# State-space scan: the exponent banks from one 96-row product each over a block-diagonal operand, copies stored as often as used, and another spacing of the banks over the steps

## The chip, the core and the metric

The kernel runs on one core of one Trainium2 chip, in one launch. The metric is the device time of that launch in microseconds (us), lower is better. The engines are TensorE (PE in the profile, its weight loads PEld), VectorE (DVE), ScalarE (ACT) and GpSimd (POOL). SyncE (SP) issues most of the DMAs. The engines run their own instruction streams and wait for each other on semaphores.

## The reference

The model adds six stages to a residual `x` of 2048 tokens by 128 features: a mixture of eight GELU experts, attention, the GELU mixture again, a mixture of eight ReLU experts, a state-space scan, and the ReLU mixture again. The change is in the scan alone (and in a memory clear inside the ReLU mixture before it). The scan, cut to what matters:

```python
x = L0_attn_x
x = x + 0.5 * _L0_ffn_ref(_layernorm(x), ...)      # GELU mixture
x = x + _L0_attn_ref(_layernorm(x), ...)
x = x + 0.5 * _L0_ffn_ref(_layernorm(x), ...)
x = x + 0.5 * _L1_ffn_ref(_layernorm(x), ...)      # ReLU mixture
x = x + _L1_attn_ref(_layernorm(x), ...)           # the scan
x = x + 0.5 * _L1_ffn_ref(_layernorm(x), ...)

def _L1_attn_ref(x, norm_w, x_proj_w, dt_proj_w, dt_proj_b, A_log, D, out_proj_w):
    xn = _rmsnorm(x, norm_w)
    proj = jnp.einsum('bld,pd->blp', xn, x_proj_w)
    delta_lo, Bs, Cs = jnp.split(proj, [DT_RANK, DT_RANK + STATE], axis=-1)
    delta = jax.nn.softplus(jnp.einsum('blr,dr->bld', delta_lo, dt_proj_w) + dt_proj_b)
    A = -jnp.exp(A_log)
    # the tokens are cut into M chunks of CHUNK = 64; all chunks are stepped at once
    def step(h, inp):
        dt, bt, ct, xt = inp
        dA = jnp.exp(dt[..., None] * A)
        h = dA * h + dt[..., None] * bt[:, None, :] * xt[..., None]
        y = jnp.einsum('mdn,mn->md', h, ct)
        return (h, y)
    _, ys = jax.lax.scan(step, jnp.zeros((M, Dm, STATE)), (dt_seq, b_seq, c_seq, x_seq))
    return jnp.einsum('bld,od->blo', y + x * D, out_proj_w)
```

## The kernel before

The scan walks 64 steps (`NSTEP`), for all chunks at once. The state lies in SBUF as 128 partitions (two batch halves of 64 state entries) by 2048 columns (16 chunks by 128 features), in three buffers `hsf`. The names `usf`, `bsf`, `decayf`, `hsf`, `cz`, `aw` and most of the staging are carved out of one tile, and the profile calls all of them `arena`; `ps` is PSUM, eight banks of 512 columns. A **step** t does this:

- *inputs* (line 1042): PE forms b times u for step t+1, sixteen 12-row products into PSUM banks 0 to 3, eight for banks 0 and 1 (`inputs(e, t+1, (0, 1))`), eight for 2 and 3. 12 rows are three bfloat16 parts paired so that the product is near fp32.
- *add_input* (2025): DVE adds PSUM to the state, 1024 columns, then 512, then 512.
- *decay_state* (2037 on DVE for the first 1024 columns, 1606 on POOL for the other two times 512): state times decay, for step t+1. DVE's order in a step is add 0, add 1, multiply of t+1, add 2.
- *state_out* (1057): PE contracts the state with c, 32 instructions, into banks 6 and 7.

Four steps are a **unit** (`TU = 4`), sixteen units in all. The decay of a unit, exp(-dt A) for 4 steps, is 128 by 8192 values in `decayf[u % 2]`. It is made in 16 **banks** of 512 columns: *spread_bank* (1029) has PE form dt times A for 8 features in PSUM bank 4 or 5, and *decay_bank* (1326) has ACT take the exponent into `decayf`. A spread waits until the exponent two banks before it is done, because only two PSUM banks take turns. Before, a bank is eight products of 64 columns, each with its own weights (`aw[0:nk, d]`, 120 rows of which 12 are not zero), and the moving operand `dts` holds 10 features in its rows for 8 steps (`TC = 8`, `DG = 10`).

The order of the work is written out by hand in `scan_tensor`, `scan_scalar`, `scan_vector` and `scan_pool`. A step of PE is: the first spread of its list, inputs of banks 0 and 1, two spreads, wait for DVE's add 2, inputs of banks 2 and 3, state_out, the rest of the list. The list has 5 banks in steps 0 to 3 and 4 afterwards, so that unit u+1 is complete after step 4u+2 and the multiply for step 4u+4, issued by DVE in step 4u+3, finds it. ACT takes the exponents in the same order, and beside them, once in a unit, `state_copy` (1344), `state_place` (1353, four small copies) and `place_c` (1337, two copies); the last two stand behind the exponents of the second step of a unit.

Before the steps, `dt`, `u` and `b` are split into three bfloat16 parts (ACT casts 1385, 1386, 1391), written to DRAM by SP (631, 634, 638, 646, 652) and read back in the row arrangement that PE wants (642, 644 and `fetch_dt` 626; `fetch_inputs` 618, 24 DMAs for four steps). They all go on one SP queue. The parts lie in memory that the scan uses again: the second `decayf` holds the parts of u and b, so that the exponents of unit 1 wait for `u_out` (line 1320 of the listing), and a state buffer lies on the parts of dt, so that the first multiply waits for `dt_out`.

```python
                sp.wait_ge(SC["dt_cast"], NPART * NTB)       # line 632
...
                sp.dma_start(scratch["dt"].rearrange("d k r n -> d (k r n)"),       # line 646
                             dtparts.rearrange("p k a b n -> p (k a b n)")).then_inc(dt_out, 16)
```

## Time and profile before

| | |
|---|---|
| time, median of 3 runs | 1384.51 us (1381.24 to 1386.95) |
| the profiled execution: span from first to last instruction | 1389.3 us |
| PE busy in the span | 1105.4 us, 80% |
| DVE busy | 939.3 us, 68% |
| ACT busy | 775.9 us, 56% |
| POOL busy | 754.5 us, 54% |
| mean granted TensorE clock, share of full speed | 0.860 |

The trace gives no other time for the profiled execution than its span. The times of a trace are counted from the first instruction. Each view groups instructions by engine and line; "idle" is the time in which the engine did nothing before an instruction, with the releaser that ended it (`<-ACT arena L1326` means that it waited for ACT's line 1326). `x16` counts instructions that stand together as one row, and the duration is then that of the group. A matmul's duration includes its way through the array, so that neighbours overlap; the distance from start to start tells what it occupies. PEclk is the granted TensorE clock: 1.00 is 2.4 GHz and 0.50 is 1.2 GHz. An idle stretch of an engine matters only where something waits for what it does next.

### The profile page before, as it was taken

The page shows a single profiled execution, that of the slowest core. Times are in us where ns is not written, and L with a number is a line of the kernel's source. Part 1 is how long each engine was busy: PE and PEld are TensorE (multiplying, and loading weights), DVE is VectorE, ACT ScalarE, POOL GpSimd, SP SyncE. Part 2 cuts the span into 40 slices and gives each one's busy share as a digit, 9 for nine tenths or more (in the row PEclk, how much of TensorE's full clock was granted, in tenths as well). Part 3 has the DMA queues.
Part 4 walks back from the last instruction along what each step waited for, and adds up shares of the span by engine and source line. Part 5 has one row for each costly group of instructions (what it writes and reads, how often), then busy time and mean ns, then how long its engine had stood idle before and what let it go on. Part 6 is the DMA issues. An engine that isn't in the chain of part 4 may idle for free. (4 is left out here: it accounts for less than half of the span.)

```text
span 1389.3 us, 26829 instructions
## 1 busy us (share of the span) xinstructions
PE 1105.4 (80%) x9728; PEld 712.6 (51%) x9728; DVE 939.3 (68%) x2104; ACT 775.9 (56%) x1511; POOL 754.5 (54%) x659
## 2 busy tenths in 40 slices
PE   5899998588888888688999969553688888884783
PEld 4677775122222222266788746322566666654562
DVE  7867867777777776478777723456578888885332
ACT  6868864136565666677877714236555665541231
POOL 4876686643332321188667661623378888781322
PEclk9999999559898979899999989775779999875896
DMA  8200000301211110011000012103311111101122
GB/s 238 67 17 1 1 1 0 61 6 26 31 31 31 32 31 0 1 61 61 1 1 1 0 60 67 51 6 119 81 38 39 41 39 40 32 14 67 58 78 65
DMA packets 92154, 55.39 MB, mean 40 GB/s; under 512 B 54253, under 2 KB 85749, under 8 KB 91128
## 3 DMA queue, kind: packets, MB, share of 16 engines
q1 hardware_dynamic: 89975, 49.48, 13.4%
q0 software_dynamic: 2048, 4.20, 1.0%
q8 instruction: 79, 1.29, 0.4%
q14 instruction: 52, 0.42, 0.1%
HBM read 31.06 MB, written 14.20 MB: 33 GB/s over the span
## 5 line engine op out<-in xcount | busy, mean ns | idle before, releaser
L1606 POOL TENSOR_TENSOR arena<-arena 128x512 f32<-128x512 f32 x126 | 214.7, 1724 | 87.0 <-ACT arena L1326 35.8
L1643 POOL TENSOR_TENSOR hr<-arena,hr 128x512 fp32r<-128x512 f32 x128 | 183.2, 1439 | 63.3 <-ACT hr L1226 61.8
L782 PE MATMUL ps<-xp,wup 128*128 128x512 f32 x768 | 196.3, 406 | 15.2 <-POOL wup L1617 8.5
L1326 ACT ACTIVATE arena<-ps 128x512 f32<-128x512 f32 x256 | 142.9, 597 | 108.1 <-PE ps L1029 103.7
L782 PE MATMUL ps<-hr,wdn 128*128 128x512 f32 x768 | 196.1, 404 | 8.2 <-issue 5.5
L1226 ACT ACTIVATE arena<-ps 128x512 f32<-128x512 f32 x256 | 160.0, 625 | 75.7 <-PE ps L782 75.4
L1282 ACT ACTIVATE arena<-ps 128x1024 f32<-128x1024 f32 (+1 forms) x192 | 149.1, 810 | 89.9 <-PE ps L935 88.7
L1892 DVE TENSOR_TENSOR hr<-arena,hr 128x512 fp32r<-128x512 f32 x128 | 132.3, 1048 | 74.3 <-ACT hr L1226 74.1
L782 PEld LDWEIGHTS ps<-xp,wup 128*128 128x128 f32 x768 | 147.2, 195 | 49.4 <-POOL wup L1617 10.7
L2025 DVE TENSOR_TENSOR arena<-arena,ps 128x1024 f32<-128x1024 f32 x189 | 154.2, 857 | 18.1 <-PE ps L1042 17.7
L782 PEld LDWEIGHTS ps<-hr,wdn 128*128 128x128 f32 x768 | 143.7, 189 | 39.0 <-issue 11.2
L1226 ACT ACTIVATE hr<-ps 128x512 fp32r<-128x512 f32 x256 | 162.1, 633 | 0.0
L1958 DVE CUSTOM_DVE_ANT_0 arena<-ps,arena 128x512 f32<-128x512 f32 (+3 forms) x256 | 112.8, 488 | 58.7 <-PE ps L920 57.3
L1527 POOL TENSOR_SCALAR_AFFINE_SELECT arena<-arena 128x512 f32<-128x512 f32 x64 | 40.9, 639 | 204.3 <-ACT arena L1282 203.7
L920 PE MATMUL ps<-arena 64*128 64x512 bf16 (+3 forms) x384 | 114.6, 394 | 40.9 <-DVE maxima L1958 15.5
L920 PEld LDWEIGHTS ps<-arena 64*128 64x128 bf16 x384 | 28.5, 99 | 173.9 <-DVE maxima L1958 94.8
L950 PE MATMUL ps<-arena 128*32 128x512 f32 (+3 forms) x768 | 93.9, 566 | 5.0 <-POOL arena L1527 5.0
L2037 DVE TENSOR_TENSOR arena<-arena 128x1024 f32<-128x1024 f32 x63 | 77.6, 1232 | 27.6 <-ACT arena L1326 27.6
L935 PE MATMUL ps<-arena 64*128 64x512 bf16 (+3 forms) x384 | 89.6, 378 | 7.9 <-ACT arena L1282 7.9
L1650 POOL TENSOR_TENSOR arena<-arena 128x512 f32<-128x512 f32 x56 | 74.3, 1327 | 36.4 <-DVE arena L1907 27.0
L1961 DVE TENSOR_REDUCE maxima<-ps 128x1 f32<-128x512 f32 x128 | 81.6, 684 | 13.6 <-PE ps L920 12.6
L1669 POOL DMA_INDIRECT arena<-ys_rows,slot_of x32 | 30.3, 947 | 101.8 <-DMA ys_rows<-arena 93.3
(239 smaller groups left out, 1885.0 us busy)
## 6 DMA issues: line engine op xcount, KB each, us to landing
arena<-up_dram SPq DMA_DIRECT2D x16, 256.0 KB, 3.0
arena<-dn_dram SPq DMA_DIRECT2D x16, 256.0 KB, 3.4
ys_rows<-arena SPq DMA_DIRECT2D x8, 320.0 KB, 2.5
arena<-up_dram SPq DMA_DIRECT2D x2, 1024.0 KB, 4.8
arena<-dn_dram SPq DMA_DIRECT2D x2, 1024.0 KB, 6.9
arena<-xs_rows SPq DMA_DIRECT2D x4, 512.0 KB, 4.8
b_parts<-arena SPq DMA_DIRECT2D x1, 1536.0 KB, 5.1
dt_parts<-arena SPq DMA_DIRECT2D x1, 1536.0 KB, 6.4
```

The lines of the kernel that those rows point to most:

```text
L782: mm = e.matmul(out, left(a), right(b), start=(first and n == 0), stop=(last and n == 2))
L920: mm = e.matmul(ps[:, n % 2, m * w:(m + 1) * w], qT[vp][rows, i, h // HP, :], kT[v % 3][rows, 4 * half:4 * half + w // P, h // HP, :], sta ...
L935: mm = e.matmul(ps[:, 2 + 2 * pair + h, 0:w], kT[v % 3][rows, j, pair, :], qm[rows, vp, pair, half * 512 + q0:half * 512 + 512], start=Tru ...
L950: mm = e.matmul(ps[32 * h:32 * h + 32, 6 + half, q0:512], vpad[:, vp, j, h, :], probT[:, n % 2, h, 0:w], start=(j == 0), stop=(w == P), sk ...
L1226: a = e.activation(to, ps[:, fc, :], ACT.Gelu)
L1282: e.activation(probT[:, m % 2, 2 * pair:2 * pair + 2, 0:w], ps[:, 2 + 2 * pair:4 + 2 * pair, 0:w], ACT.Exp, scale=SCALE).then_inc(AT["exp_ ...
L1326: e.activation(to, ps[:, 4 + n % 2, :].rearrange("p (d m t) -> p t m d", d=DBK, t=TU), ACT.Exp, scale=-1.0).then_inc(SC["decay_ready"], 1)
L1606: e.tensor_tensor(hsf[t % 3][:, cols], decayf[u % 2][:, t4 * W + cols.start:t4 * W + cols.stop], hsf[(t - 1) % 3][:, cols], ALU.mult).then ...
L1643: e.tensor_tensor(hr[:, i % 2, 1, fc, :], hid[:, i % 2, fc, :], hr[:, i % 2, 0, fc, :], ALU.subtract).then_inc(MX["rest_pool"], 1)
L1892: e.tensor_tensor(hr[:, i % 2, 1, fc, :], hid[:, i % 2, fc, :], hr[:, i % 2, 0, fc, :], ALU.subtract).then_inc(MX["rest_vector"], 1)
L1958: ins = e.tensor_tensor_reduce(masked_s[n % 2][:, m * w:(m + 1) * w], of, causal[:, 4 * P - w:4 * P], 1.0, MASKED, ALU.add, ALU.max, to)
L2025: e.tensor_tensor(to, to, of, ALU.add).then_inc(SC["added"], 1)
```

## The change

- *A bank is one product.* Bank g of a unit holds the features 8g to 8g+7. The moving operand `dts` of a bank is now 96 rows (8 features by 12 rows, `BR`) by 512 columns, block-diagonal: feature l's 12 rows are filled in the columns of feature l alone and are zero elsewhere. The weights `aw[0:96, g]` hold the 8 features under each other. One matmul of 512 columns takes the place of eight of 64.
- *dt is fetched per unit.* `fetch_dt(u)` is 8 DMAs of 12 rows by 16 banks by 64 elements, in two slots that were both cleared before (the clear in the ReLU mixture covers `dts` now, and no longer all of `aw`). Before, `fetch_dt(k)` was 30 DMAs for two units, and the first read (642, 644) filled two units.
- *Rows are stored as often as used.* The DRAM copies of dt, u and b have 12 rows in place of 6: parts 0 to 2, 0 to 1 and 0 are written one after the other (`for c0, na in RUNS`). So each of these stores is 3 DMAs and twice the bytes (u twice 3), and a read is one DMA per row group: `fetch_inputs` is 8 DMAs in place of 24, of the same bytes.
- *Spacing.* `ahead_at(t)` gives a step's list: 5, 5, 5, 1 over the steps of a unit (6 in step 0). In the last step of a unit the one bank stands behind state_out. On ACT `state_place` and `place_c` move to the last step of the unit, ahead of its exponent.

The core of the diff:

```diff
-        aw = carve(D * P // 2).bitcast(BF16).rearrange("p (d n) -> p d n", n=P)
-        dts0 = carve(NDG * NM * TC // 2)
+        awf = carve(BKU * P // 2)
+        aw = awf.bitcast(BF16).rearrange("p (g n) -> p g n", n=P)
+        dtsf = carve(2 * BKU * 512 // 2)
+        dts = dtsf.bitcast(BF16).rearrange("p (s g n) -> p s g n", s=2, g=BKU)
+        assert top[0] == CLEARED
...
                 def fetch_inputs(k):
                     for r in range(RG):
                         m2, hh = r // 2, r % 2
+                        for to, name, landed in ((usf, "u", u_in), (bsf, "b", b_in)):
+                            of = scratch[name][m2, TI * k:TI * (k + 1), :, hh, :]
...
+                            sp.dma_start(to[k % 2][32 * r:32 * r + KR].rearrange("p (t n) -> p t n", t=TI),
+                                         of.rearrange("t r n -> r t n")).then_inc(landed[k % 2], 16)
...
+                def fetch_dt(u):
+                    for dl in range(DBK):
+                        sp.dma_start(dts[KR * dl:KR * (dl + 1), u % 2, :, dl * NM * TU:(dl + 1) * NM * TU],
+                                     scratch["dt"][dl::DBK, u].rearrange("g r n -> r g n")).then_inc(dt_in[u % 2], 16)
+
+                def put_dt(u0, u1, landed):
+                    for c0, na in RUNS:
+                        sp.dma_start(scratch["dt"][:, u0:u1, 2 * c0:2 * c0 + 2 * na, :].rearrange("d u r n -> d u (r n)"),
+                                     dtparts[:, u0:u1, 0:na].rearrange("p k a b n -> p k (a b n)")).then_inc(landed, 16)
+
+                def put_u(t0, t1, landed):
+                    for m2 in range(2):
                         for c0, na in RUNS:
-                            rows = slice(32 * r + 2 * c0, 32 * r + 2 * c0 + 2 * na)
-                            for to, name, a0, landed in ((usf, "u", 0, u_in), (bsf, "b", NPART - na, b_in)):
-                                of = scratch[name][m2, TI * k:TI * (k + 1), a0:a0 + na, :, hh, :]
-                                sp.dma_start(to[k % 2][rows].rearrange("p (t n) -> p t n", t=TI),
-                                             of.rearrange("t a b n -> (a b) t n")).then_inc(landed[k % 2], 16)
-
-                def fetch_dt(k):
-                    for dg in range(DG):
-                        ng = len(range(dg, D, DG))
-                        for c0, na in RUNS:
-                            r0 = KR * dg + 2 * c0
-                            sp.dma_start(dts[k % 2][r0:r0 + 2 * na, 0:ng, :],
-                                         scratch["dt"][dg::DG, k, 0:2 * na, :].rearrange("g r n -> r g n")
-                                         ).then_inc(dt_in[k % 2], 16)
+                            sp.dma_start(scratch["u"][m2, t0:t1, 2 * c0:2 * c0 + 2 * na].rearrange("t r h n -> t (r h n)"),
...
+                put_dt(0, 2, dt0_out)
...
+                put_u(0, TI, stored)
                 sp.wait_ge(dt0_out, 16 * len(RUNS))
...
+                sp.wait_ge(SC["zeroed"], 2)
+                fetch_dt(0)
+                sp.wait_ge(b_out, 16 * len(RUNS))
+                sp.wait_ge(stored, 16 * U_STORES)
                 fetch_inputs(0)
...
+                put_dt(2, NUN, dt_out)
+                put_u(TI, CHUNK, u_out)
+                fetch_dt(1)
+                sp.wait_ge(u_out, 16 * 2 * len(RUNS))
                 fetch_inputs(1)
-                sp.wait_ge(dt_out, 16)
-                sp.wait_ge(SC["xn_turned"], NTB)
-                fetch_dt(1)
-                for k in range(2, NI):
-                    sp.wait_ge(SC["in_done"], 3 * TI * (k - 1))
-                    fetch_inputs(k)
-                    if k % 2 == 0 and k // 2 + 1 < NC:
-                        sp.wait_ge(SC["spread_done"], 2 * BKU * (k // 2))
-                        fetch_dt(k // 2 + 1)
+                sp.wait_ge(dt_out, 16 * len(RUNS))
+                for k in range(1, NI):
+                    if k >= 2:
+                        sp.wait_ge(SC["in_done"], 3 * TI * (k - 1))
+                        fetch_inputs(k)
+                    if k + 1 < NUN:
+                        sp.wait_ge(SC["spread_done"], BKU * k)
+                        fetch_dt(k + 1)
...
         def spread_bank(e, n):
 
-            u, q = unit_of(n)
-            k, th = u * TU // TC, u % (TC // TU)
-            if q == 0 and th == 0:
-                e.wait_ge(dt_in[k % 2], 16 * 2 if k == 0 else 16 * (2 - 2 * (k % 2) + DG * len(RUNS) * ((k + 1) // 2)))
+            u, g = unit_of(n)
+            if g == 0:
+                e.wait_ge(dt_in[u % 2], 16 * DBK * (u // 2 + 1))
             if n >= 2:
                 e.wait_ge(SC["decay_ready"], n - 1)
-            for j in range(DBK):
-                d = q * DBK + j
-                nk = KR * min(DG, D - d // DG * DG)
-                of = dts[k % 2][0:nk, d // DG, :].rearrange("p (m t) -> p m t", t=TC)
-                mm = e.matmul(ps[:, 4 + n % 2, j * 64:(j + 1) * 64], aw[0:nk, d, :],
-                              of[:, :, th * TU:(th + 1) * TU], start=True, stop=True)
-            mm.then_inc(SC["spread_done"], 1)
+            e.matmul(ps[:, 4 + n % 2, :], aw[0:BR, g, :], dts[0:BR, u % 2, g, :], start=True, stop=True).then_inc(SC["spread_done"], 1)
+
+        def ahead_at(t):
+
+            first = 0 if t == 0 else 5 * (t % TU) + 1
+            first += BKU * (t // TU + 1)
+            return [n for n in range(first, first + (6 if t == 0 else 1 if t % TU == TU - 1 else 5)) if n < NUN * BKU]
...
-            ahead = BKU
             for t in range(NSTEP):
-                todo = [n for n in range(ahead, ahead + (5 if t < 4 else 4)) if n < NUN * BKU]
-                ahead += len(todo)
-                for n in todo[0:1]:
+                todo = ahead_at(t)
+                last = t % TU == TU - 1
+                for n in todo[0:1] if not last else ():
                     spread_bank(e, n)
                 if t + 1 < NSTEP:
                     e.wait_ge(SC["added"], 3 * t + 1)
                     inputs(e, t + 1, (0, 1))
-                for n in todo[1:2]:
-                    spread_bank(e, n)
-                for n in todo[2:3]:
+                for n in todo[1:3] if not last else ():
                     spread_bank(e, n)
                 e.wait_ge(SC["added"], 3 * t + 3)
                 if t + 1 < NSTEP:
                     inputs(e, t + 1, (2, 3))
                 state_out(e, t)
-                for n in todo[3:]:
+                for n in todo if last else todo[3:]:
...
+                u, t4 = t // TU, t % TU
+                todo = ahead_at(t)
+                if t4 == TU - 1:
+                    if u >= 1:
+                        state_place(e, u - 1)
+                        if u + 1 < NUN:
+                            place_c(e, u + 1)
+                for n in todo[0:3]:
                     decay_bank(e, n)
-                if t % TU == 0 and t > 0:
-                    state_copy(e, t // TU - 1)
-                for n in todo[2:]:
+                if t4 == 0 and u >= 1:
+                    state_copy(e, u - 1)
+                for n in todo[3:]:
                     decay_bank(e, n)
-                if t % TU == 1 and t > TU:
-                    state_place(e, t // TU - 1)
-                    if t // TU + 1 < NUN:
-                        place_c(e, t // TU + 1)
...
-                        e.memset((czf, aw)[b], 0.0).then_inc(SC["zeroed"], 1)
+                        e.memset(arena[:, 0:CLEARED - 2 * BKU * 512 // 2] if b == 0 else dtsf, 0.0).then_inc(SC["zeroed"], 1)
...
-    shapes = {"dt": (D, NC, NPART * B, NM * TC), "u": (2, CHUNK, NPART, B, 2, 4 * D), "b": (2, CHUNK, NPART, B, 2, 4 * P), "dt0": (D, KR, NM * TC),
+    shapes = {"dt": (D, NUN, KR, NM * TU), "u": (2, CHUNK, KR, 2, 4 * D), "b": (2, CHUNK, KR, 2, 4 * P), "ap": (NPART, D, STATE)}
```

What this makes of the order. PE of the kernel before, from the inputs of banks 2 and 3 in the second step of a unit's spreads (t = 4u+1) to state_out of step 4u+3 (L1029 spread, L1042 inputs, L1057 state_out; eight L1029 are one bank; the profile counts each L1057 twice):

```order
L1042 MATMUL ps<-arena 128x128 x8
L1057 MATMUL ps<-arena 32x128 x16
L1029 MATMUL ps<-xn,arena 128x64 x16
L1042 MATMUL ps<-arena 128x128 x8
L1029 MATMUL ps<-xn,arena 128x64 x16
L1042 MATMUL ps<-arena 128x128 x8
L1057 MATMUL ps<-arena 32x128 x16
L1029 MATMUL ps<-xn,arena 128x64 x16
L1042 MATMUL ps<-arena 128x128 x8
L1029 MATMUL ps<-xn,arena 128x64 x16
L1042 MATMUL ps<-arena 128x128 x8
L1057 MATMUL ps<-arena 32x128 x16
```

The last bank of unit u+1 is the first eight of the sixteen L1029 behind the second of the three L1057 (that of step 4u+2). The same place in the changed kernel, from state_out of step 4u+1 (L1022 spread, one row is one bank, L1039 inputs, L1054 state_out):

```order
L1054 MATMUL ps<-arena 32x128 x16
L1022 MATMUL ps<-arena 128x512 x3
L1039 MATMUL ps<-arena 128x128 x8
L1022 MATMUL ps<-arena 128x512 x2
L1039 MATMUL ps<-arena 128x128 x8
L1054 MATMUL ps<-arena 32x128 x16
L1022 MATMUL ps<-arena 128x512 x2
L1039 MATMUL ps<-arena 128x128 x16
L1054 MATMUL ps<-arena 32x128 x16
L1022 MATMUL ps<-arena 128x512 x2
L1039 MATMUL ps<-arena 128x128 x8
```

Behind state_out of step 4u+2 stand two banks now (the last two of unit u+1), and then nothing but inputs until state_out of step 4u+3, behind which the first bank of unit u+2 follows, together with that of the next step.

ACT over a little more than a unit, before (L1326 exponent, L1344 state_copy, L1353 state_place, L1337 place_c):

```order
L1326 ACTIVATE arena<-ps 128x64x8 x10
L1344 COPY arena<-ps 128x128
L1326 ACTIVATE arena<-ps 128x64x8 x6
L1353 COPY xnT<-ps 128x8x4 x4
L1337 COPY arena<-arena 64x4x16 x2
L1326 ACTIVATE arena<-ps 128x64x8 x10
```

and in the changed kernel (L1320, L1338, L1347, L1331 in the same order):

```order
L1320 ACTIVATE arena<-ps 128x64x8 x12
L1347 COPY xnT<-ps 128x8x4 x4
L1331 COPY arena<-arena 64x4x16 x2
L1320 ACTIVATE arena<-ps 128x64x8 x4
L1338 COPY arena<-ps 128x128
L1320 ACTIVATE arena<-ps 128x64x8 x12
```

The small copies stood between the sixth and the seventh last exponents of a unit and now stand behind its last one.

SP's queue at the start of the scan, before (L642 and L644 read dt of units 0 and 1, L646 stores dt, L618 reads u and b):

```order
L638 DMA u_parts<-arena 4x6144 [waits scan_u_cast]
L638 DMA u_parts<-arena 4x6144
L642 DMA arena<-dt_parts 120x12x128 [waits dt0_out]
L644 DMA arena<-dt_parts 96x128
L646 DMA dt_parts<-arena 128x6144
L618 DMA arena<-u_parts 6x4x512 [waits stored,b_out]
L618 DMA arena<-b_parts 6x4x512
```

followed by the other 22 L618, the rest of u (L652, two rows of 60x6144) and the L618 of the next four steps. In the changed kernel, behind the eight reads L616 of the first four steps:

```order
L616 DMA arena<-b_parts 12x4x512
L626 DMA dt_parts<-arena 128x14x384
L626 DMA dt_parts<-arena 128x14x256
L626 DMA dt_parts<-arena 128x14x128
L632 DMA u_parts<-arena 60x6144
L632 DMA u_parts<-arena 60x4096
L632 DMA u_parts<-arena 60x2048
L632 DMA u_parts<-arena 60x6144
L632 DMA u_parts<-arena 60x4096
L632 DMA u_parts<-arena 60x2048
L621 DMA arena<-dt_parts 12x16x64 x8
L616 DMA arena<-u_parts 12x4x512 [waits u_out]
```

The read of dt for unit 1 (the eight L621) now stands behind the stores of all the rest of dt (L626) and of u (L632).

## Rows read from the trace of the kernel before

**Rows 1.** windows: stretch, length, busy (count) of each engine, PEclk, DMA share, GB/s

```profile
1023.60:1249.00 225.40, 188.20 (x4300) 144.66 (x4300) 193.53 (x221) 129.99 (x304) 187.50 (x110) 0.87 0.13 34
```

**Rows 2.** waits from 984 to 1255 us: total us, times, longest

```profile
DVE arena L2037 <- ACT arena L1326: 27.6, 15, 2.4
```

**Rows 3.** timeline of DVE: start, duration, engine, line, what, count [idle before, releaser]

```profile
1208.82 1.22 DVE L2037 TENSOR_TENSOR arena<-arena 128x1024 f32<-128x1024 f32 x1
...
1212.28 1.23 DVE L2037 TENSOR_TENSOR arena<-arena 128x1024 f32<-128x1024 f32 x1
...
1215.76 1.22 DVE L2037 TENSOR_TENSOR arena<-arena 128x1024 f32<-128x1024 f32 x1
...
1222.05 1.22 DVE L2037 TENSOR_TENSOR arena<-arena 128x1024 f32<-128x1024 f32 x1 [2.35 <-ACT arena L1326]
```

**Rows 4.** timeline of DVE, the first multiply of unit 2 and of unit 15

```profile
1023.59 1.23 DVE L2037 TENSOR_TENSOR arena<-arena 128x1024 f32<-128x1024 f32 x1 [2.13 <-ACT arena L1326]
...
1238.41 1.23 DVE L2037 TENSOR_TENSOR arena<-arena 128x1024 f32<-128x1024 f32 x1 [2.02 <-ACT arena L1326]
```

**Rows 5.** timeline of all engines over one step

```profile
1108.80 1.22 DVE L2037 TENSOR_TENSOR arena<-arena 128x1024 f32<-128x1024 f32 x1
...
1110.67 0.40 PE L1042 MATMUL ps<-arena 12*128 12x128 bf16 x8
...
1110.99 1.08 PE L1057 MATMUL ps<-arena 128*32 128x128 f32 x32
...
1112.01 0.41 PE L1029 MATMUL ps<-arena 120*128 120x64 bf16 x8
...
1112.46 2.19 ACT L1326 ACTIVATE arena<-ps 128x512 f32<-128x512 f32 x4 [1.10 <-PE ps L1029]
...
1113.11 0.90 PE L1029 MATMUL ps<-arena 120*128 120x64 bf16 x16
```

**Rows 6.** timeline of ACT and PE near the end of a unit

```profile
1100.51 0.64 ACT L1337 COPY arena<-arena 64x64 f32<-64x64 f32 x2
...
1101.83 0.41 PE L1029 MATMUL ps<-xn,arena 120*128 120x64 bf16 x8 [1.22 <-ACT arena L1326]
```

**Rows 7.** the windows view, two idle stretches of PE and two slow ones

```profile
1083.80:1085.10 1.30, 0.11 (x4) 0.00 (x0) 1.30 (x3) 1.24 (x4) 1.30 (x2) 1.00 0.17 38
...
1085.80:1089.20 3.40, 3.40 (x61) 2.64 (x58) 0.94 (x2) 1.26 (x3) 0.65 (x2) 0.50 0.18 42
...
1117.00:1118.20 1.20, 0.00 (x0) 0.00 (x0) 1.20 (x2) 1.15 (x4) 1.20 (x2) 1.00 0.21 52
...
1184.80:1198.40 13.60, 12.99 (x217) 10.09 (x205) 9.73 (x12) 5.91 (x12) 10.26 (x6) 0.50 0.12 36
```

**Rows 8.** timeline of PE in the first steps

```profile
987.06 1.94 PE L1057 MATMUL ps<-arena 128*32 128x128 f32 x32
```

**Rows 9.** the timeline of SP; a DMA row spans its issue alone

```profile
966.32 0.42 SPq L646 DMA_DIRECT2D dt_parts<-arena  x1
...
977.36 0.77 SPq L652 DMA_DIRECT2D u_parts<-arena  x2
```

**Rows 10.** DMA view from 950 to 986 us: size of each, us to landing

```profile
dt_parts<-arena SPq DMA_DIRECT2D x1, 1536.0 KB, 6.4
u_parts<-arena SPq DMA_DIRECT2D x2, 720.0 KB, 6.3
```

**Rows 11.** timelines of ACT, DVE and PE, the first unit

```profile
985.33 1.08 ACT L1326 ACTIVATE arena<-ps 128x512 f32<-128x512 f32 x2 [3.06 <-DMA u_parts<-arena]
...
999.06 1.22 DVE L2037 TENSOR_TENSOR arena<-arena 128x1024 f32<-128x1024 f32 x1 [2.36 <-ACT arena L1326]
...
1004.82 1.03 PE L1029 MATMUL ps<-xn,arena 120*128 120x64 bf16 x16 [6.09 <-DMA xn<-dt_parts]
```

**Rows 12.** the timeline of PE in the first mixture, products of 512 columns

```profile
99.66 2.67 PE L782 MATMUL ps<-hr,wdn 128*128 128x512 f32 x11
102.16 2.20 PE L782 MATMUL ps<-xp,wup 128*128 128x512 f32 x9
```

73 lines of the change are left out of this document (25 added, 48 removed).

## The prediction

> **What bounds the kernel now.** I read the windows view over the scan first, then the waits, then the timelines of DVE, PE and ACT over a few units, then the start of the scan on SP's queue. Outside the scan the change touches only a clear on POOL, so only the scan counts.
>
> Over the steps from the eighth multiply on, DVE is busy for 193.5 of 225.4 us and PE for 188.2 [rows 1]. The reader is to see that neither is full, so that the time sits in a pattern. The timeline of DVE shows it: from multiply to multiply a step takes 3.46 us (1208.82 to 1212.28), with no idle time, but the fourth takes 6.29 (1215.76 to 1222.05), with 2.35 of waiting for the last exponent of the next unit [rows 3]. DVE waits so 15 times, for 27.6 us in all [rows 2]. From the first multiply of unit 2 to that of unit 15, 13 units take 1238.41 - 1023.59 = 214.8 us, 16.52 each [rows 4]. Three steps of 3.46 leave 6.1 for the fourth in the mean. A step cannot be shorter than 3.46, since DVE's own work fills it; so the change can win at most 2.7 us in a unit, and only at that place.
>
> Why is the last exponent late? One step in order: the multiply starts at 1108.80 and PE's inputs of banks 2 and 3 at 1110.67, 1.87 later, when DVE's add 2 is over. State_out starts at 1110.99, so inputs occupy 0.32, and the next spread at 1112.01, so state_out occupies 1.02 [rows 5]. ACT starts 0.45 behind that spread, at 1112.46, and an exponent takes 0.60 (PE has the first bank back at 1113.11) [rows 5]; DVE follows at once. Sum from the multiply: 1.87 + 0.32 + 1.02 + 0.45 + 0.60 + 0.04 = 4.30 us, against the 3.46 at which DVE wants it. On top of that the six small copies of ACT stand right before those last exponents, and PE waits 1.22 us for ACT [rows 6]. Last, the clock: PE stood idle for 1.2 us of the stretch from 1083.8 to 1085.1 at PEclk 1.00, and from 1085.8 on it had 0.50, 1.2 GHz [rows 7]. At that clock state_out takes 1.94 us in place of 1.08 [rows 8], just where the last bank waits behind it.
>
> **The change part by part.**
>
> *Eight products of 64 columns become one of 512.* The eight of a bank last 0.41 us from the first start to the last end [rows 5]. For one of 512 columns the nearest rows are the mixture's: 11 in 102.16 - 99.66 = 2.50 us, 0.227 each from start to start; the last of them runs on 0.17 behind the next start (99.66 + 2.67), so that one lasts 0.40 [rows 12]. PE is free earlier, by less than 0.41 - 0.227 = 0.18 us a bank, but what ACT waits for is the end, 0.41 against 0.40. I cost it at 0; at the bounds the path gets 0.1 us a unit shorter or longer.
>
> *Order: 5, 5, 5, 1.* The list of the third step still ends behind state_out, and now with two banks. The second exponent starts 0.50 us after the first (four take 2.19 us, so (2.19 - 0.60) / 3 = 0.53 apart, less where nothing is waited for, rows 5), so the sum of above is 4.30 + 0.50 = 4.80 us. Before it, each five-bank step has its own round: inputs 0.32, state_out 1.02, spread to ACT 0.45, exponent 0.60, back to PE 0.05, the third bank's 0.43 and 0.60 and 0.05, and the last spread 0.22, in all 3.74. That is 0.28 over DVE's step; two such rounds bring PE 0.5 us late to the inputs of the third step. DVE does not stall yet, since its add 0, as long as a multiply, runs while PE makes these inputs. The fourth step is then 4.80 + 0.5 = 5.3 us at full clock, the unit 3 x 3.46 + 5.3 = 15.7.
>
> *The six copies* go where ACT has nothing to do; their 1.22 us wait of PE is gone. That gain is in the 5.3 already: with it, the kernel before had about 5.2 at full clock, so that the two edits of the order cancel: -0.9 for the copies, +0.5 for the second bank, +0.5 for the rounds.
>
> *A longer idle stretch of PE.* In the last step of a unit nothing is left to spread before state_out. From the next to last spread S on, the multiply starts at S + 0.45 + 0.50 + 0.60 + 0.04 = S + 1.6, while PE is done with the last spread and inputs 0 and 1 at S + 0.22 + 0.22 + 0.32 = S + 0.8. Its next work, inputs of banks 2 and 3, comes 1.87 behind the multiply: 2.7 us idle, twice the stretches of rows 7. Of the two shown there one was followed by 1.2 GHz and one was not; with 2.7 I expect it in nearly every unit. What 1.2 GHz costs: in the slow stretch of 13.6 us PE was busy for 13.0 and DVE for 9.7, so PE was the bound [rows 7]. In the new order the slow stretch begins behind the idle time and, like most, lasts 3.4 us (1085.8 to 1089.2). In it two inputs at 0.6, state_out at 1.9, three spreads at 0.43 (twice the full-clock figures) and a wait for an exponent come to 4.6 us, against 3.46 and some 0.5 of slack behind add 0: one step is 0.6 to 0.8 longer, and 0.3 of it is carried to the fourth. Unit: 15.7 + 0.8 + 0.3 = 16.8. In some units it lasts for a second stretch and costs another 1.2; I take 17.0. Against 16.52: +0.5 for 13 units, +6 us. Bounds: 15.7 (never slow), -11 us; 17.9 (always two), +18 us.
>
> *The start of the scan.* Unit 1's exponents need `u_out`. Before, SP issued the rest of dt at 966.32 and the rest of u at 977.36 [rows 9]; ACT went on at 985.33 [rows 11]. The store of dt took 6.4 us for 1536 KB [rows 10], that of u 985.33 - 977.36 = 8.0 for 1440 KB. Now 2688 KB of dt and 2880 KB of u are written, one behind the other, and the read of dt for unit 1 stands behind both. SP reaches them some four to five us later than 966.3 (18 short issues come before), which is 970.5. dt: 6.4 x 2688 / 1536 = 11.2, u: twice 8.0 less the fixed part of about 1.5, 14.5, which is 996.2; the read lands about 1 us behind that, 997. PE, whose next instruction is the spread of unit 1's first bank, stands there, and behind it the inputs of step 1, so DVE and POOL stand too. Before, the fourth multiply came 999.06 - 985.33 = 13.7 us after the exponents of unit 1 could start [rows 11]; the same puts it at 1010.7, 11.7 late. Then the next read is no longer late: PE's 6.09 us wait for unit 2's dt [rows 11] goes, since the read is issued a unit ahead. From there to the first multiply of unit 2 it took 1023.59 - 999.06 = 24.5 us [rows 4, 11]; now about one unit, 17. Net 11.7 - 7.5 = +4. Bounds: both stores at dt's rate and the read hidden, -3; the small pieces (256 bytes in the last store) at half rate, +12.
>
> On small pieces the Trainium skill (DMA: Bandwidth & Descriptors, the table at its head) says that below 512 bytes the DMA engine reads, modifies and writes. No row here shows a store in pieces of 256 bytes. If the 448 KB in such pieces cost double, my estimate by that page and the dt row is 2 us more.
>
> *The rest.* SP has fewer issues in the loop and was waiting for PE there; the clear on POOL has as many bytes and stands between waits for stores; the casts write runs of 4 in place of 8. All at 0, bounds 0 to +2 us together for the casts.
>
> **Sum.** +4 at the start, +6 in the loop: +10 on the profiled 1389.3 us span. The median of the runs is 4.8 us under that span, so 1384.5 + 10 = 1394.5 us.
>
> **The rivals.** A change within 0.5% (6.9 us) cannot be told from none here.
>
> 1. *The clock holds, and the fourth step is shorter* (faster). If PE's idle stretch is followed by 1.2 GHz in few units, a unit is 15.7: -11 in the loop, +4 at the start, so 1378. For it: 1.20 us of idle at 1117 had no consequence [rows 7]. Against: it is twice as long now. The Trainium skill (TensorE: Matmul & The Clock Gate, "Why this matters for your kernels") sides with this rival: the idle gaps it tells one to avoid are longer than 2.7 us. The trace disagrees already at 1.3 us. Chance 0.14.
> 2. *The wait is truly gone* (the change does more than I read): every step 3.46, -2.7 x 13 + 4, 1354. It would need the last bank to be spread before state_out, which the order excludes. Chance 0.02.
> 3. *A wash*: slow stretches cost what they cost before (16.5 a unit) and the start +0 to +6: 1387. Chance 0.24.
> 4. *1.2 GHz stays for whole units* (slower): PE at that clock needs 2 x 0.6 + 1.9 + 5 x 0.43 = 5.3 us for a five-bank step, and the gap of the fourth step renews it. From the point at which it covers two steps in most units, a unit is 17.9 or more: +18 + 4, and with the casts 1408. Row 1184.8 shows such a stretch once in before. Chance 0.12.
>
> The forecast, a slow step in each unit and a late start, has 0.48. Faster by over 0.5%: 0.14 + 0.02 less a little that falls short, 0.15. Slower: 0.12, 0.40 of the forecast's 0.48 and 0.05 of the wash, 0.57. Within: 0.28. The range for 8 in 10 reaches down to the first rival's side and up to the fourth: 1380 to 1409; the likeliest case alone 1389 to 1401.
>
> **What would show it.** In the changed profile: DVE's multiplies at 3.46, 3.46, 4.3 and 5.5 us, the last with a wait for ACT of 1.5 to 2 us; a 2.7 us idle stretch of PE in every unit, PEclk 0.50 behind it; no 6.09 us wait for dt in unit 1, but one of more than 10 us before the second step, and ACT's first exponent of unit 1 at about 996. The forecast is wrong if PEclk stays 1.00 over the loop (rival 1), if the stores of dt and u land before 990, or if the fourth step is under 4.8 us.

## The result, and the profile after

| | before | changed |
|---|---|---|
| time, median | 1385.1 us (4 runs) | 1462.4 us (4 runs, 1452.4 to 1464.2) |
| ratio, with 95% interval | | 1.052 (1.046 to 1.058) |
| the profiled execution, span | 1389.3 us | 1460.7 us |
| mean granted clock of the span | 0.860 | 0.807 |

The change makes the kernel 5.2% slower. The medians lie 77 us apart and the profiled spans 71, where 10 were forecast. The direction was right, the size was not.

The windows view over the stretch of [rows 1] (length, busy time and count of PE, PEld, DVE, ACT and POOL, PEclk, DMA share, GB/s), and below it one 1.2 GHz stretch and the full-clock stretch that follows it:

```profile
1023.60:1249.00 225.40, 195.63 (x2299) 99.03 (x2299) 156.96 (x175) 107.67 (x247) 147.97 (x88) 0.61 0.21 29
...
1105.40:1136.10 30.70, 27.73 (x303) 14.14 (x303) 21.86 (x25) 12.25 (x28) 20.58 (x13) 0.50 0.27 29
1136.10:1146.35 10.25, 7.44 (x117) 3.70 (x115) 6.91 (x9) 7.58 (x18) 6.32 (x5) 1.00 0.09 26
```

The granted clock fell from 0.87 to 0.61. DVE got 175 instructions done in place of 221, while PE was busy for longer, 195.6 against 188.2 us. From 1064.4 to 1310 us the same two stretches, 30.7 us at 1.2 GHz and 10.2 at full speed, take turns. Of the two stretches of 1.2 GHz in [rows 7], the one like most others there lasted 3.4 us.

DVE's multiplies over two units (start, duration, what, idle before and releaser):

```profile
1107.58 1.22 DVE L2031 TENSOR_TENSOR arena<-arena 128x1024 f32<-128x1024 f32 x1
1112.12 1.22 DVE L2031 TENSOR_TENSOR arena<-arena 128x1024 f32<-128x1024 f32 x1
1117.86 1.22 DVE L2031 TENSOR_TENSOR arena<-arena 128x1024 f32<-128x1024 f32 x1
1126.53 1.23 DVE L2031 TENSOR_TENSOR arena<-arena 128x1024 f32<-128x1024 f32 x1 [2.84 <-ACT arena L1320]
1130.00 1.22 DVE L2031 TENSOR_TENSOR arena<-arena 128x1024 f32<-128x1024 f32 x1
1134.54 1.22 DVE L2031 TENSOR_TENSOR arena<-arena 128x1024 f32<-128x1024 f32 x1
1139.46 1.22 DVE L2031 TENSOR_TENSOR arena<-arena 128x1024 f32<-128x1024 f32 x1
1145.07 1.23 DVE L2031 TENSOR_TENSOR arena<-arena 128x1024 f32<-128x1024 f32 x1 [1.71 <-ACT arena L1320]
```

The steps take 4.54, 5.74, 8.67, 3.47 and then 4.54, 4.92, 5.61 us; in [rows 3] three of four took 3.46. The last exponent is still what ends the wait, as the prediction said, but at 1.2 GHz the steps ahead of it are longer too. Thirteen units from the first multiply of unit 2 to that of unit 15, which answer to [rows 4], take 264.2 us, 20.33 each:

```profile
1044.66 1.23 DVE L2031 TENSOR_TENSOR arena<-arena 128x1024 f32<-128x1024 f32 x1 [2.84 <-ACT arena L1320]
```

```profile
1308.90 1.23 DVE L2031 TENSOR_TENSOR arena<-arena 128x1024 f32<-128x1024 f32 x1 [1.71 <-ACT arena L1320]
```

PE's idle stretches of a unit's last step, in its timeline, with the fall of the clock at 1146.35 inside the last of them:

```profile
1105.99 0.61 PE L1039 MATMUL ps<-arena 12*128 12x128 bf16 x8 [2.49 <-DVE arena L2019]
...
1128.41 0.61 PE L1039 MATMUL ps<-arena 12*128 12x128 bf16 x8 [2.07 <-DVE arena L2019]
...
1146.95 0.61 PE L1039 MATMUL ps<-arena 12*128 12x128 bf16 x8 [2.49 <-DVE arena L2019]
```

And the start, in the timelines of SP, PE and ACT. SP spends 5.3 us on the six issues of u's first part, comes to the rest of dt at 976.7 and to the rest of u at 983.3; the read of dt for unit 1 takes it 7.6 us to issue:

```profile
963.53 5.33 SPq L632 DMA_DIRECT2D u_parts<-arena  x6
...
976.71 6.55 SPq L626 DMA_DIRECT2D dt_parts<-arena  x3
983.30 12.78 SPq L632 DMA_DIRECT2D u_parts<-arena  x6
```

```profile
996.11 7.63 SPq L621 DMA_DIRECT2D arena<-dt_parts  x8
```

```profile
1005.21 0.61 PE L1022 MATMUL ps<-arena 96*128 96x512 bf16 x1 [18.32 <-DMA arena<-dt_parts]
```

```profile
1005.94 0.60 ACT L1320 ACTIVATE arena<-ps 128x512 f32<-128x512 f32 x1 [18.97 <-PE ps L1022]
```

The first exponent of unit 1 starts at 1005.94, in [rows 11] at 985.33. The first multiply of unit 2 comes 21.1 us later than before (1044.66 against 1023.59) and that of unit 15 70.5 us later (1308.90 against 1238.41). So 21 us are lost at the start and 49.4 in thirteen units, together 70.5 of the 71.4 us by which the span grew.

### The profile page after: what moved, and what is told of

It is laid out like the page before. It is cut to its first block and busy times, and to the rows that moved or that the text cites. A ratio compares the mean times of both kernels' runs of the same rounds, so it can differ in the third digit from the quotient of the medians.

```text
span 1460.7 us, 22914 instructions
## 1 busy us (share of the span) xinstructions
PE 1155.8 (79%) x7936; PEld 676.7 (46%) x7936; DVE 944.9 (65%) x2104; ACT 775.1 (53%) x1511; POOL 746.8 (51%) x659
## 5 line engine op out<-in xcount | busy, mean ns | idle before, releaser
L1600 POOL TENSOR_TENSOR arena<-arena 128x512 f32<-128x512 f32 x126 | 213.9, 1716 | 158.0 <-DVE arena L2019 61.2
L1320 ACT ACTIVATE arena<-ps 128x512 f32<-128x512 f32 x256 | 140.5, 595 | 176.2 <-PE ps L1022 175.4
L2019 DVE TENSOR_TENSOR arena<-arena,ps 128x1024 f32<-128x1024 f32 x189 | 158.6, 861 | 72.7 <-PE ps L1039 72.5
L780 PE MATMUL ps<-xp,wup 128*128 128x512 f32 x768 | 193.3, 401 | 15.0 <-POOL wup L1611 8.2
L780 PE MATMUL ps<-hr,wdn 128*128 128x512 f32 x768 | 195.8, 404 | 10.2 <-issue 7.6
L1022 PE MATMUL ps<-arena 96*128 96x512 bf16 x256 | 119.9, 541 | 34.7 <-DMA arena<-dt_parts 22.2
L1054 PE MATMUL ps<-arena 128*32 128x128 f32 x2048 | 111.8, 389 | 0.1
L1039 PE MATMUL ps<-arena 12*128 12x128 bf16 x1024 | 69.2, 277 | 35.1 <-DVE arena L2019 35.0
```

The lines of the kernel that those rows point to most:

```text
L780: mm = e.matmul(out, left(a), right(b), start=(first and n == 0), stop=(last and n == 2))
L1022: e.matmul(ps[:, 4 + n % 2, :], aw[0:BR, g, :], dts[0:BR, u % 2, g, :], start=True, stop=True).then_inc(SC["spread_done"], 1)
L1054: mm = e.matmul(ps[32 * ml:32 * ml + 32, 6 + u % 2, 0:D], cz[:, u % 2, ml, (4 * mh + t4) * 32:(4 * mh + t4 + 1) * 32], hsf[t % 3][:, m * D ...
L1320: e.activation(to, ps[:, 4 + n % 2, :].rearrange("p (d m t) -> p t m d", d=DBK, t=TU), ACT.Exp, scale=-1.0).then_inc(SC["decay_ready"], 1)
L1600: e.tensor_tensor(hsf[t % 3][:, cols], decayf[u % 2][:, t4 * W + cols.start:t4 * W + cols.stop], hsf[(t - 1) % 3][:, cols], ALU.mult).then ...
L2019: e.tensor_tensor(to, to, of, ALU.add).then_inc(SC["added"], 1)
```

## The experiments

The median of the kernel before lay between 1367 and 1390 us on the chips of the experiments, so ratios are compared, and times of a trace. Behind each expectation stands the measured ratio to the kernel before, with its 95% interval in brackets. "Unit" is the mean of the thirteen units from the first multiply of unit 2 to that of unit 15, in us, and "stretches" are those at 1.2 GHz behind the start. The diffs are cuts. First come the two parts of the change and the form of the product.

**The product alone, in the order before.** The changed kernel with the lists and ACT's copies of before:

```diff
-            first = 0 if t == 0 else 5 * (t % TU) + 1
-            first += BKU * (t // TU + 1)
+            first = BKU + (5 * t if t < 4 else 20 + 4 * (t - 4))
...
```

> The changed kernel with the lists 5, 5, 5, 5, then 4 in each step, one bank on each side of the inputs, and the small copies of ACT where they were before; the one wide product and the new stores stay. Theory 'spacing' (the 2.5 us idle stretch of the last step and two banks behind state_out make the loop slow): the units go back to about 16.5 us, the slow stretches to 3.4 us, and only the late start stays, so about 1385 + 19 = 1404 us. Theory 'form' (with wide products PE does not get its clock back at 1.2 GHz, whatever the order): units stay near 20 us with slow stretches over 20 us, about 1450 us.

1.038 (1.033 to 1.044), unit 19.47, stretches of up to 44.4 us. "Spacing" fails as the only cause. The windows view of 14.3 us at 1.2 GHz in which PE is busy throughout (such a stretch is there three times):

```profile
1180.40:1194.70 14.30, 14.30 (x156) 7.26 (x156) 11.00 (x13) 5.93 (x16) 11.28 (x8) 0.50 0.19 16
```

**The new order alone, in the kernel before.** The rest of the order, on PE and on ACT, is that of the change too.

```diff
-                todo = [n for n in range(ahead, ahead + (5 if t < 4 else 4)) if n < NUN * BKU]
+                todo = ahead_at(t)
+                last = t % TU == TU - 1
...
```

> The kernel before with the lists 6, 5, 5, 1, then 5, 5, 5, 1 and the moved copies of ACT; eight products of 64 columns, its own stores. Theory 'spacing': units of about 20 us, slow stretches over 20 us, first start as before, so about 1435 us. Theory 'form': the clock falls in every unit but is back after one 3.4 us stretch, as my sum had it: units of 16.5 to 17, 1385 to 1395 us.

1.029 (1.024 to 1.034), unit 20.48, every one with 13.7 us at 1.2 GHz and 6.8 at full clock:

```profile
1023.60:1249.00 225.40, 193.14 (x3538) 148.70 (x3536) 158.43 (x178) 109.07 (x253) 149.68 (x89) 0.67 0.12 31
```

"Form" fails as the only cause too: each part alone makes the clock stay low, and the order alone, over the 120 rows of before, already gives units as long as the change's 20.33.

**Eight products of 64 columns on the new operand.**

```diff
-            e.matmul(ps[:, 4 + n % 2, :], aw[0:BR, g, :], dts[0:BR, u % 2, g, :], ...)
+            for j in range(8):
+                mm = e.matmul(ps[:, 4 + n % 2, j * 64:(j + 1) * 64], aw[0:BR, g, :],
+                              dts[0:BR, u % 2, g, j * 64:(j + 1) * 64], start=True, stop=True)
```

> The changed kernel with a bank formed by eight products of 64 columns over the same 96 rows and the same operand (the same weights eight times), everything else as changed. Theory 'form': slow stretches of 3.4 to 7 us in place of 30.7, units near 17, about 1405 us. Theory 'spacing': no difference from the changed kernel, 1455 to 1470 us.

1.045 (1.042 to 1.049), unit 20.38 against 20.33, the same 30.7 us stretches. In this order the width of the product does not matter. With the order of before as well:

> The changed kernel with both undone that can be undone apart from the data: the order of the kernel before, and eight products of 64 columns a bank. What is left of the change is the 96-row block-diagonal operand and the stores with their late start. Theory 'order or width' (either the wide product or the new order keeps the clock low): about 1385 + 18 = 1403 us, slow stretches of 3.4 us, units of 16.5. Theory 'operand' (what the rows hold matters, or something that the late start sets off): units over 18 and slow stretches over 10 us, as in the kernel with the order of before and the wide product, about 1450 us.

1.052 (1.046 to 1.059), unit 19.92. The one wide product in this order had 1.038 and 19.47, on another chip. Of these 1.4% the traces show 0.45 us a unit, 6 us in thirteen; where the rest lies stays open. Now PE runs the same instructions in the same order as before, but over 96 rows in place of 120 and with one set of weights for the eight. What is left is the operand and the start.

**The idle stretch filled.** Products of no use in the last step of a unit:

```diff
+                if last and todo:
+                    e.wait_ge(SC["decay_ready"], todo[0] - 1)
+                    for _ in range(18):
+                        e.matmul(ps[:, 4, 0:2 * D], aw[0:BR, 0, :], aw[0:BR, 0:2, :], start=True, stop=True)
                 e.wait_ge(SC["added"], 3 * t + 3)
```

> The changed kernel with 18 products of 256 columns, of no use, in the last step of each unit between the inputs of banks 0 and 1 and those of 2 and 3, into the PSUM bank that is written anew behind them. At full clock they last about 2.1 us and fill the idle stretch, at 1.2 GHz about 3.9 us. If the idle stretch is what drops the clock, and nothing else does, it stays at 1.00 once it has come back: units near 16, 1462 - 13 x 4.5 = about 1405 us. If the clock falls for another reason, the filler only costs, 1.5 to 3 us in each unit: 1480 to 1500 us.

1.003 (0.999 to 1.008). The windows view of it, behind the rise of the clock at 1029.7:

```profile
1033.09:1249.00 215.91, 193.18 (x3105) 109.83 (x3106) 190.83 (x218) 135.26 (x313) 185.33 (x110) 1.00 0.23 37
```

The clock does not fall again before the end of these units, and the unit is 15.87 us. Work of no use takes the kernel from 1.052 to 1.003. The idle stretch of the last step is what drops the clock. Two multiplies around that step:

```profile
1101.66 1.22 DVE L2035 TENSOR_TENSOR arena<-arena 128x1024 f32<-128x1024 f32 x1
...
1107.13 1.23 DVE L2035 TENSOR_TENSOR arena<-arena 128x1024 f32<-128x1024 f32 x1 [1.71 <-ACT arena L1324]
```

With half of the filler:

> The changed kernel with 9 filler products of 256 columns in place of 18, so that some 1.0 us of the 2.5 us idle stretch is filled. Theory 'idle stretch': what is left, about 1.5 us, is like the stretches of the kernel before, behind which the clock fell in some of the units: between 1394 and 1462 us, about 1425. If 1.5 us is short enough to do no harm, it is 1390 to 1395 us; if any idle stretch over 1 us drops the clock, 1450 us or more.

1.040 (1.033 to 1.046), unit 19.30, stretches of 30.7 us again in the middle of the loop: half a filling keeps the clock up in few units.

**Rows.** First the kernel before with 8 features in the rows in place of 10. The first read of dt is also cut into two DMAs of another shape:

```diff
-DG = 10
+DG = 8
...
```

> The kernel before with 8 features in the rows of dts in place of 10, so that each product of a bank spans 96 rows in place of 120; same products, same order, same bytes. No instruction of PE gets longer or shorter. Theory 'rows' (at 1.2 GHz the chip weighs what PE does by the rows that a product spans; the stretches behind which the clock came back held less of state_out, 128 rows, where the spreads had 120 rows than where they had 96): slow stretches of 7 to 40 us in place of 3.4, units near 19 to 20, so 3 to 4% over before, some 45 us. Rival 'zeros or data' (only the block-diagonal operand, three quarters of which and more are zeros, does it): no change, within 0.5% of before.

1.041 (1.034 to 1.047), unit 20.30. PE's products and their order are those of before, no wait was added, and 52 us are lost. The windows view, beside [rows 1]:

```profile
1023.60:1249.00 225.40, 203.85 (x3590) 158.51 (x3587) 159.85 (x178) 111.73 (x256) 149.87 (x89) 0.61 0.12 31
```

Then the changed kernel over 128 rows, the added ones all zeros, in the order of before:

```diff
-            e.matmul(ps[:, 4 + n % 2, :], aw[0:BR, g, :], dts[0:BR, u % 2, g, :], ...)
+            e.matmul(ps[:, 4 + n % 2, :], aw[:, g, :], dts[:, u % 2, g, :], ...)
...
```

> The changed kernel in the order of before, with its wide product over 128 rows in place of 96; rows 96 to 127 of both operands are zeros, so the values are the same. Theory 'rows': the clock comes back after one or two short stretches, as in the kernel before; from 1.038 of before to about 1.012, which is the late start alone (some 17 us). Rival 'zeros or data': more zeros change nothing or make it worse, 1.035 to 1.04.

1.006 (1.002 to 1.010) in place of 1.038, unit 16.17, stretches of 3.4 us, two of 6.8:

```profile
1023.60:1249.00 225.40, 174.36 (x2859) 97.57 (x2911) 195.66 (x224) 130.86 (x307) 189.29 (x112) 0.89 0.24 35
```

The same edit in the changed order:

> The changed kernel with the wide product over 128 rows, rows 96 to 127 zeros. Theory 'rows': the idle stretch still drops the clock in every unit, but it comes back sooner, about as in the kernel with the new spacing alone (120 rows, slow for 13.7 of 20.5 us): units of 20.5 or less in place of 20.5 in the mean of 18.5 and 22.4, with the late start 1.035 to 1.045 of before, against 1.052 for 96 rows. Rival 'zeros or data': 1.05.

1.014 (1.007 to 1.021) in place of 1.052, unit 17.11. That is far better than expected: the expectation took 128 rows to be like the 120 of the new order alone, whose unit is 20.48. The two differ by 8 rows, but also in the form (one wide product in place of eight) and in what the rows hold, and no run parts these. And the order of before, with one row more than the change has:

> The changed kernel in the order of before, with the wide product over 97 rows: one row of zeros more than in the change. If the clock goes by the number of rows: as with 96 rows, 1.038 of before, slow stretches up to 40 us. If it goes by groups of 32 rows that a product touches: as with 128 rows, 1.006 of before, slow stretches of 3.4 us mostly.

1.034 (1.025 to 1.043), unit 18.87: near the 96 rows (1.038, 19.47) and far from the 128 (1.006, 16.17). So it does not go by the groups of 32 rows that a product touches.

**The start.** The read of dt for unit 1 ahead of the stores, on the kernel with the filled gap:

```diff
                 fetch_dt(0)
+                fetch_dt(1)
...
                 put_u(TI, CHUNK, u_out)
-                fetch_dt(1)
```

> The kernel with the filled gap (18 products) and the read of dt for unit 1 issued right behind that of unit 0, ahead of the stores of the rest of dt and u. It takes only the part of the late start that comes from the place of this read. PE waited for it until 1005.2, while the store of u landed at 1002.65, on which ACT waits: the loop starts 2 to 2.5 us earlier, and the first bank of unit 1 is spread long before. 1394 - 2 = 1392 us. A rival: this read was the whole delay, and the loop starts as early as before, 1375 us.

1.006 (1.002 to 1.011), which can't be told from 1.003. In the trace ACT now waits for u_out, 19.29 us, and the fourth multiply comes 30.6 us behind the first in place of 34.3; but the clock rises for good 4.9 us later behind the first multiply, and from the first multiply to the eighth it is 51.0 against 51.8. And u in 6 rows:

```diff
-                        for c0, na in RUNS:
-                            sp.dma_start(scratch["u"][m2, t0:t1, 2 * c0:2 * c0 + 2 * na]...
+                        sp.dma_start(scratch["u"][m2, t0:t1].rearrange("t r h n -> t (r h n)"), ...
```

> The kernel with the filled gap and the early read of dt, with u stored in 6 rows, 1440 KB in place of 2880, and read in three DMAs a row group, as before. If the doubled store of u makes the rest of the late start, the first unit is 8 to 11 us shorter than in the kernel with the early read alone (35.6 us), and the time 1.0063 - 10/1368 = 0.999 of before. If the doubled store of dt does it, nothing changes.

Its runs scatter (1373.9 to 1395.7 us) and give no ratio. In the trace ACT waits 13.24 us for u, and from the first multiply to the fifth it is 6.4 us shorter (29.1 against 35.6), less than the 8 to 11 expected. ACT still waits for u, whose store stands behind the doubled one of dt; no run takes that store back.

**The changed kernel, mended**: its order and its wide product kept, over 128 rows, with both edits of the start.

> The changed kernel with its order 5, 5, 5, 1 and its wide product, but over 128 rows, the early read of dt and u in 6 rows. If rows and start explain the whole loss of 5.2%: 1.0137 less 10 to 13 us of start, 1.004 to 1.007, which is what my sum said of the loop alone (+6 us). If the spacing costs more by itself: over 1.015.

1.0047 (1.001 to 1.009), unit 17.04, as expected. So 128 rows and the two edits of the start undo nearly the whole loss in the changed order. This does not give the 96 rows their share in it, since 128 are more than the 120 of before, and the same order over 120 rows has a unit of 20.48.

**A version that beats both.** The kernel before with the last bank of each unit ahead of state_out, and with ACT's small copies in the last step of a unit:

```diff
-                todo = [n for n in range(ahead, ahead + (5 if t < 4 else 4)) if n < NUN * BKU]
+                todo = [n for n in range(ahead, ahead + (5 if t < 5 else 4)) if n < NUN * BKU]
...
```

> The kernel before (eight products, its own stores) with five banks in the first five steps in place of four, so that the last bank of every unit is the third of its list and stands ahead of state_out, and with ACT's small copies in the last step of a unit, behind the last exponent. If the wait of 2.35 us for the last exponent is gone and nothing takes its place, 15 units lose up to 2.7 us each: 1389 - 35 = 1350 us at full clock, and the idle stretch of PE, which was part of the same wait, goes too. If PE, which needs some 3.3 us of each 3.46, is the bound through its waits for ACT: about 1370 us. If the clock falls more often: over 1400.

0.981 (0.974 to 0.989), unit 15.16; 0.91 of the full clock. The same order in the changed kernel, with the wide product over 128 rows and both edits of the start:

> What the runs point to, together: one wide product per bank over 128 rows; five banks in the first five steps and four afterwards, so that the last bank of a unit stands ahead of state_out; the small copies in a unit's last step; the read of dt for unit 1 ahead of the later stores; u stored in 6 rows and read in three DMAs, as before. The step is then bound by DVE's 3.46 us. If the clock holds (PE is busy for some 2.6 of 3.46 us, with no idle stretch over 0.7 us): units of 13.9 to 14.3, a start a few us behind that of before: 0.97 of before. If PE's spare time drops the clock in most steps: units of 16 to 18, about 1.00.

0.982 (0.976 to 0.987), unit 14.82. Its trace shows where the rest is, in the last step of a unit: ACT's six copies, and PE behind them:

```profile
1156.24 0.45 ACT L1350 COPY xnT<-ps 128x32 f32<-128x32 f32 x4
...
1156.71 0.63 ACT L1334 COPY arena<-arena 64x64 f32<-64x64 f32 x2
...
1158.02 0.39 PE L1025 MATMUL ps<-arena 128*128 128x512 bf16 x1 [1.24 <-ACT arena L1323]
```

So the copies are spread over three steps:

```diff
+                if t % TU == 1 and t > TU:
+                    state_place(e, t // TU - 1)
+                if t % TU == 2 and t > TU and t // TU + 1 < NUN:
+                    place_c(e, t // TU + 1)
                 for n in todo[3:]:
                     decay_bank(e, n)
...
```

> The fastest so far with ACT's small copies split over three steps, each ahead of the exponent that waits for state_out, where ACT stands idle for 0.9 to 1.3 us. In that kernel the third spread of the last step waits 1.24 us for ACT, which comes out of the copies late, and the step takes 3.90 us: if that is all, 15 x 0.43 = 6 us less, 0.977 of before. If ACT is late at another place then: no change, 0.9815.

0.976 (0.967 to 0.984), and in a second, longer run:

> The fastest kernel once more, for a tighter ratio and as the partner of the next one: 0.97 to 0.98 of before.

0.976 (0.971 to 0.982). So this kernel is faster than the one before by 1.8 to 2.9%. The windows view of the first of the two runs:

```profile
1023.60:1202.00 178.40, 158.70 (x2699) 82.72 (x2703) 178.40 (x207) 126.65 (x299) 173.05 (x104) 1.00 0.20 44
```

DVE is busy for 178.40 of 178.40 us: the unit is 13.85, four steps of 3.46, which is what the second rival of the prediction asked for. This kernel over 96 rows:

> The same with the product over 96 rows. If rows matter only while the clock is at 1.2 GHz: equal units of 13.84 us once it is up, and a later rise at the start, 0 to 10 us slower in all. If 96 rows also let the clock fall at full speed, where PE is busy for some 2.5 of 3.46 us: slow stretches throughout and 3 to 5% more than its partner.

0.980 (0.974 to 0.986), not to be told from its partner by the ratios. The windows view has both halves of the matter:

```profile
1035.00:1063.00 28.00, 28.00 (x304) 14.27 (x305) 21.30 (x24) 13.53 (x31) 18.55 (x12) 0.50 0.17 37
1064.00:1222.00 158.00, 140.96 (x2405) 73.45 (x2401) 157.84 (x183) 112.55 (x267) 152.33 (x92) 1.00 0.19 42
```

At 1.2 GHz PE is busy for 28.00 of 28.00 us, and the clock does not come. Once it is up, at 1063.3 (the two over 128 rows had it for good at 1012.3 and 1026.6), it stays, with units of 13.85. The traced execution took 1375.9 us, where the six of this kernel lie between 1351.8 and 1377.0, so how late the rise is rests on a single trace. That a fully busy PE can stay at 1.2 GHz does not: the 14.30 of 14.30 us above show it too.

The units, by order and rows (us). All at 120 rows are eight products, all at 97 and 128 one wide product:

| order | 96 rows | 97 | 120 | 128 |
|---|---|---|---|---|
| of before | 19.47, 19.92 (eight products), 20.30 (kernel before) | 18.87 | 16.52 | 16.17 |
| 5, 5, 5, 1 | 20.33 (the change), 20.38 (eight products) | | 20.48 | 17.11, 17.04 (mended) |
| last bank ahead of state_out | | | 15.16 | 14.82 |
| the same, copies split | 14.58 (13.85 once up) | | | 13.85 |

## Why the prediction was wrong

*What bounds the kernel* held: there is one place, the last exponent of a unit, behind which DVE waits. Taking it away gave a distance of 3.46 us in every step.

*One product in place of eight, costed at 0.* In duration this was right: at the same rows and in the changed order the two forms have the same unit (20.38 and 20.33). But I weighed the operand by its columns alone. That it spans 96 rows in place of 120 I had read in the diff and priced at nothing. In the order of before the rows alone make the unit 20.30 in place of 16.52. In the changed order they show no such cost: with eight products it is 20.48 over 120 rows and 20.38 over 96. So this term was wrong, but the loop would have missed its forecast by as much without it.

*The order.* The fourth step was to be 5.3 us at full clock, the unit 15.7; with the gap filled they are 5.47 and 15.87. What the order costs at full clock was sized right as a sum; its terms were not measured apart.

*The idle stretch.* The forecast was 2.7 us with 1.2 GHz behind it in nearly every unit. Measured are 2.49 and 2.07, and the clock falls in every second unit, only because it is still low in the others. The filler shows the cause. The step that failed is the length of what follows: "like most, lasts 3.4 us". It lasts 30.7, and 13.7 in each unit where the rows are still 120. The 3.4 us were what the trace shows of the order of before; I carried them over to another order, in which the slow stretch begins behind a longer idle time. Where the rows are 128, the stretches of the changed order are 3.4 or 6.8 us and the unit is 17.11, near the 17.0 of the sum; but neither kernel had 128 rows, so that is no proof of the sum. The term is mis-sized by 20.33 - 17.0 = 3.3 us a unit, 43 us in thirteen.

*The start* was forecast at +4 and measured at +21. The stores were priced right: dt from 976.71 to 988.0 is 11.3 us (11.2 forecast), u from there to 1002.65 is 14.6 (14.5). So the 2 us more that the pieces of 256 bytes might have cost are not in the sum. Three things were priced wrong. SP reached the stores at 976.7 and not at 970.5, 6.2 us late, most of it because the six issues of u's first part take 5.3 us where two took 0.6 before. The read of dt ends 2.6 us behind u and not 0.8, its eight issues taking 7.6 us behind the stores. With the 0.7 us from there to ACT's first exponent and 0.2 of the stores, that makes 8.9, 1005.9 against 997. And what follows runs at 1.2 GHz for the most part, 16.3 against 13.7 us up to the fourth multiply and 22.4 against 17 for the next unit (8.0). 8.9 + 8.0 is the 17 that are missing. 43 + 17 = 60 of the 61 us by which the span was missed.

*The rivals.* The fourth, 1.2 GHz for whole units, is nearest to what happened. It had 0.12 and was priced at 17.9 a unit, since I took it for two slow steps, where all of them and the wait for the last exponent grow (8.67 us). What spoke for it was in the trace: at 1184.8 to 1198.4 PE was busy for 12.99 of 13.60 us and the clock did not come back [rows 7]. I set it aside as the odd one. It was the sign that a busy PE does not by itself get its clock back. The first rival, that the clock holds, is refuted for the change and true with the filler.

The Trainium skill (TensorE: Matmul & The Clock Gate, "What's actually happening") says that the clock follows how busy PE has recently been. For the fall the filler agrees. For the rise the rows disagree: 28.00 of 28.00 us busy at 0.50, and 4.1% of the time for 24 rows fewer in the same instructions. The measurement decides.

## What to carry to other kernels

Read the granted clock beside the busy time of every stretch, and before shrinking what PE does ask where its idle time will lie: here work of no use in one idle stretch took the kernel from 1.052 to 1.003. A product padded with rows of zeros takes no longer (0.39 us at full clock over 96 and over 128 rows) and here brought the clock back sooner (1.052 to 1.014 from that alone). And a duration that the trace shows for a state, such as the length of a slow stretch, belongs to the work that ran in it; it is a bound for other work only when that work and its order are unchanged.

## What the runs showed of the hardware

- At 1.2 GHz full occupation in the records is not enough for the clock to rise; with the same instructions in the same order, 96 rows gave 209 us of 264 at 1.2 GHz, 120 rows 48 of 215 (the thirteen units of the kernel before, in its two forms). In a stretch over 128 rows, 3.07 of 3.40 us busy came just ahead of full clock (1105.8 to 1109.2 in the changed kernel over 128 rows).
- Rows that hold only zeros count as rows (128 against 96: unit 16.17 against 19.47), and one row more than 96 helps little (18.87, stretches still up to 44.4 us). In the order 5, 5, 5, 1 there was no gain from 96 to 120 rows (20.38 and 20.48, eight products in both) and a large one at 128 (17.11). Between 97 and 120 rows nothing was tried, nor was the number of rows of the inputs (12) changed. Why it is so stays open; only that it is so is shown.
- 96 rows are enough to hold the clock where no long idle stretch comes: it stayed at 1.00 from 1063.3 on for 158 us with PE busy for 141 of them, and for 216 us with the gap filled. Whether the rows matter for the fall behind an idle stretch is not shown.
- A DMA issue is not always short: the six stores of u's rest take SP 12.8 us to issue, and the eight reads behind them 7.6 (the first two 2.4 each), where reads of the same size take about 0.39 each later in the loop. That a full queue is the reason is likely from their place behind 5.6 MB of stores, but not shown.
